# A scan kernel on one Trainium2 core: silu of two operands made 45 steps apart, projection tiles placed over the whole of a unit, D times xs made by GpSimd in place

## The chip, the core and the metric

One core of a Trainium2 chip runs the whole kernel. The metric is the device time of one execution in microseconds; the time of the kernel before is the median of three runs. The core has TensorE (PE, matmuls, with its weight loads PEld), VectorE (DVE), ScalarE (ACT), GpSimd (POOL) and SyncE (SP, which issues the DMAs); each works through its own list of instructions in program order, and they wait for one another on semaphores.

## The reference

Two batches of 1024 tokens of width 256 go through a layer with a selective scan in both directions and an MLP, and then through an attention layer with its MLP. The change touches the scan alone:

```python
xz = h @ in_w
xs, z = jnp.split(xz, 2, axis=-1)
xs = jax.nn.silu(xs)
proj = xs @ xproj_w
dt = jax.nn.softplus(proj[..., :D_INNER] + dt_bias)
Bm = proj[..., D_INNER:D_INNER + D_STATE]
Cm = proj[..., D_INNER + D_STATE:]
A = -jnp.exp(A_log)
def step(hst, ins):
    dt_t, B_t, C_t, x_t = ins
    dA = jnp.exp(dt_t[:, :, None] * A)
    hst = hst * dA + (dt_t * x_t)[:, :, None] * B_t[:, None, :]
    y_t = jnp.einsum('bds,bs->bd', hst, C_t)
    return (hst, y_t)
...
y = jnp.swapaxes(ys, 0, 1) + xs * Dskip
return y * jax.nn.silu(z) @ out_w
```

D_INNER is 512 (four groups of 128 partitions, index f), D_STATE is 64.

## The kernel before, in words

The scan is cut into 8 **units**: two directions, two batches, two halves of 512 tokens. Every second unit (1, 3, 5, 7; `hi` in the code) goes on from the state of the one before; the others start from zero. A unit has 64 **steps** `st`, one for each state; step number over all units is `w`. In each step:

- ScalarE makes four decays exp(dt x A) of 128x512 (L1091) and, between them, three copies of dtx (transposed) scaled by B for the step behind (L1073).
- TensorE turns them back into PSUM banks 4, 5 and 6 (L1652, a matmul with a diagonal that holds B, and three transposes at L1655, for each f), and adds the products of step w - 2 into banks 0 to 3 (L1661, four transposes for each f): `turn_u` and `reduce_state` in the loop at L1691.
- VectorE scans 512 tokens for each f (L1319), as soon as the decay and the PSUM bank are there. It may write step w only when TensorE has reduced step w - 3 (`RING`).
- GpSimd multiplies the scanned states by C, two f at a time (L789, 128x1024).

Beside it the **tiles** of the next unit are prepared: input path `xs` and gates `zs` (4 tiles each, 2 products each), `bc` (B and C rows, 4 products), `bT` (B turned), `dt` (4 tiles of 4 products), `dtxT` (4), and of the unit before `yT` (4) and `out` (2 tiles of 4 products). A table `TURN[u]` made by `place_turns` (L262) says at which step TensorE begins a tile; it issues one product, or one group of four transposes, in each step after f = 1 (L1700), so that a tile of four products takes four steps. All these tiles have the single PSUM bank 7 (L428), and a tile's first matmul waits until the tile before it in the bank has been copied out (`take`, `free_bank`). The copies are placed by the same table: `act_turns` (L303) puts ScalarE's copy at the end of ScalarE's step `back` = `EVICT` steps behind the start (2 for xs and zs, 3 for dt, 1 for yT, bT and dtxT), behind all decays of that step; it waits for the tile's last product. For a dt tile (L888, L889) exp follows after 4 steps (L899) and ln after 5 (L903), and GpSimd finishes dt after 6 (L766) and multiplies by xs at `DTX_STEPS` (L773). `bc` is copied by VectorE (L1200), `out` is added to x by VectorE (L1217).

In the units 1 to 6 the old table begins at step 4 with xs, yT, zs in turn (to 23), then bc 25, bT 29, dt 31, 35, 39, 43, out 47, dtxT 52, 54, 56, 58 and out 60. Once a unit, at step 24, ScalarE loads the silu table, makes silu of all xs (L919) and of all gates (L920), 128x2048 each, and loads the exp and ln table again (L1097).

D times xs comes in at a unit's first state: `first_state` (L1672) multiplies xs by a diagonal `skip_w` that holds D (L1681, fp32) for each f and c, as the first matmuls into banks 0 to 3, once VectorE has gated the unit before out of the bank (`gate_y`, L1302, in steps 1 and 2). `skip_weights` (L944) makes the eight diagonals on ScalarE at the start.

## Time and profile before

| | |
|---|---|
| median of 3 runs | 3275.02 us (3272.62 to 3275.12) |
| the profiled execution, its own time | 3272.75 us |
| its span in the profile | 3270.9 us |
| share of the span busy: PE, DVE, ACT, POOL | 98%, 88%, 86%, 71% |
| mean granted TensorE clock | 0.993 of full speed |
| first scan to last scan | 63 to 2549 us |

The profile gives for each instruction its start, its duration and the idle time of its engine before it, with the instruction that ended it in brackets. Instructions of one engine overlap a little (a scan of 1.2 us is followed by the next 1.11 us later), so what a thing costs in a full stretch is read from start to start, and short waits inside the overlap don't appear as idle time. A row of a timeline is: start (us from the span's start), us, engine, line, operation, out<-in, shapes, count, and in brackets the idle time before it and what ended it. A row of the groups by line is: line, engine, operation, names, shapes, count | busy us, mean ns of one | idle us before them, and what ended it. Matmul ends are modelled, so TensorE's busy share says little.

### The profile page before, as it was taken

What the parts mean: (1) busy time and instruction counts of PE and PEld (TensorE: products, weight loads), DVE (VectorE), ACT (ScalarE), POOL (GpSimd) and SP (SyncE); (2) the same over time, 40 slices, a digit from 0 to 9 for tenths busy, and PEclk for the clock granted to TensorE, in tenths of its full rate; (3) what the DMA queues carried; (4) which work ended last, traced back from release to release, by engine and by line L of the source; (5) the groups of instructions that cost most, each with busy time, mean ns of one, the idle gap of its engine ahead of it and who ended that gap; (6) DMA issues with size and microseconds to landing.
All of it is one profiled execution on the core that took longest, in us unless ns stands there. A gap on an engine that the chain in (4) does not pass through costs nothing.

```text
span 3270.9 us, 59384 instructions
## 1 busy us (share of the span) xinstructions
PE 3194.7 (98%) x22634; PEld 2505.6 (77%) x22634; DVE 2866.5 (88%) x2863; ACT 2815.5 (86%) x4659; POOL 2327.7 (71%) x1113
## 2 busy tenths in 40 slices
PE   8999999999999999999999999999999999999899
PEld 5888898999899998999998999999888542222244
DVE  3999999999999999999999999999999578888121
ACT  6999999999999999999999999999989436777620
POOL 1899999999999999999999999999878220000000
PEclk8999999999999999999999999999999999999999
DMA  3223222212222222222222222222212043422000
GB/s 121 69 84 81 80 72 69 72 67 72 69 73 93 70 70 75 72 69 72 73 73 74 67 72 67 74 68 71 86 57 69 29 102 59 77 34 31 15 7 20
DMA packets 199837, 218.82 MB, mean 67 GB/s; under 512 B 79969, under 2 KB 149601, under 8 KB 199297
## 3 DMA queue, kind: packets, MB, share of 16 engines
q1 hardware_dynamic: 199554, 215.02, 23.1%
q8 instruction: 180, 2.95, 0.4%
q14 instruction: 103, 0.84, 0.1%
HBM read 194.29 MB, written 18.19 MB: 65 GB/s over the span
## 4 chain that ended last, share of the span: by engine, by line
PE 76%; ACT 15%; DVE 6%; issue 3%; DMA 0%; POOL 0%; DVEq 0%; ACTq 0%; SPq 0%
PE psum L1661 21%; PE psum L1429 17%; PE psum L1655 16%; PE psum L1652 12%; ACT arena L1091 6%; ACT arena L1073 5%; PE psum L1739 4%; PE psum L1728 3%; DVE arena L1319 2%; PE psum L1712 2%; DVE row_max L1382 2%; PE psum L1681 1%; ACT arena L1116 1%; ACT arena L1076 0%; ACT arena L920 0%
## 5 line engine op out<-in xcount | busy, mean ns | idle before, releaser
L1319 DVE TENSOR_TENSOR_SCAN arena<-arena,psum 128x512 f32<-128x512 f32 x2048 | 2373.8, 1230 | 58.6 <-PE psum L1655 45.6
L789 POOL TENSOR_TENSOR arena<-arena 128x1024 f32<-128x1024 f32 x1024 | 2225.8, 2185 | 257.1 <-DVE arena L1319 233.5
L1091 ACT ACTIVATE arena<-arena,a_neg 128x512 f32<-128x512 f32 x2048 | 1442.9, 724 | 45.4 <-PE psum L1655 44.9
L1661 PE MATMUL psum<-ident,arena 128*128 128x128 f32 x8192 | 1231.9, 273 | 1.7 <-POOL arena L789 1.7
L1073 ACT ACTIVATE arena<-arena,bT 128x512 f32<-128x512 f32 x1536 | 1110.7, 723 | 0.0
L1655 PE MATMUL psum<-ident,arena 128*128 128x128 f32 x6144 | 1009.8, 273 | 0.0
L1661 PEld LDWEIGHTS psum<-ident,arena 128*128 128x128 f32 x8192 | 962.7, 141 | 2.1 <-POOL arena L789 2.1
L1652 PE MATMUL psum<-arena 128*128 128x128 f32 x4096 | 821.1, 282 | 31.8 <-ACT arena L1073 16.5
L1652 PEld LDWEIGHTS psum<-arena 128*128 128x128 f32 x4096 | 648.3, 191 | 246.6 <-issue 151.9
L1655 PEld LDWEIGHTS psum<-ident,arena 128*128 128x128 f32 x6144 | 744.2, 142 | 0.0
L1429 PE MATMUL psum<-arena 128*128 128x512 f32 (+1 forms) x1440 | 672.0, 587 | 5.2 <-DVE arena L1191 2.9
L1429 PEld LDWEIGHTS psum<-arena 128*128 128x128 f32 x1440 | 248.7, 192 | 172.4 <-issue 163.8
L1116 ACT ACTIVATE arena<-psum 128x512 f32<-128x512 f32 x512 | 267.2, 604 | 108.1 <-PE psum L1728 108.1
L1382 DVE TENSOR_REDUCE row_max<-psum 128x1 f32<-128x512 f32 x512 | 317.0, 682 | 44.8 <-PE psum L1712 44.1
L833 POOL TENSOR_TENSOR arena<-arena 128x512 f32<-128x512 f32 x8 | 10.2, 1274 | 385.5 <-DMA arena<-sums_dram 385.5
L1728 PEld LDWEIGHTS psum<-arena 100*128 100x128 bf16 x512 | 39.3, 97 | 179.1 <-ACT arena L1116 155.4
L1728 PE MATMUL psum<-arena 100*128 100x512 bf16 x512 | 160.4, 386 | 8.6 <-ACT arena L1116 6.6
L1712 PE MATMUL psum<-arena 97*128 97x512 bf16 x512 | 157.8, 386 | 6.6 <-DVE row_max L1382 6.6
L1739 PE MATMUL psum<-arena 128*32 128x512 f32 x1024 | 136.4, 604 | 4.6 <-ACT skip_w L1106 4.5
L1012 ACT ACTIVATE arena<-psum,b_up 128x512 f32<-128x512 f32 x32 | 22.0, 687 | 101.9 <-PE psum L1429 101.9
L1712 PEld LDWEIGHTS psum<-arena 97*128 97x128 bf16 x512 | 50.6, 99 | 67.9 <-DVE row_max L1382 22.3
L1233 DVE SCALAR_TENSOR_TENSOR arena<-psum,b_up,arena 128x512 f32<-128x512 f32 x32 | 24.0, 751 | 75.0 <-PE psum L1429 75.0
(118 smaller groups left out, 871.9 us busy)
## 6 DMA issues: line engine op xcount, KB each, us to landing
arena<-bc_dram SPq DMA_DIRECT2D x256, 512.0 KB, 3.7
arena<-diag_dram SPq DMA_DIRECT2D x224, 128.0 KB, 2.1
arena<-qk_dram SPq DMA_DIRECT2D x96, 128.0 KB
diag_dram<-arena SPq DMA_DIRECT2D x32, 256.0 KB, 4.4
qk_dram<-arena SPq DMA_DIRECT2D x8, 768.0 KB, 3.4
arena<-in_x SPq DMA_DIRECT2D x4, 512.0 KB, 10.5
arena<-skip_w SPq DMA_DIRECT2D x64, 32.0 KB, 2.0
arena<-sums_dram SPq DMA_DIRECT2D x64, 32.0 KB, 1.8
```

The costliest lines, as they stand in the source:

```text
L789: pool.tensor_tensor(out[:, :, way], h_now[:, :, way], c_row, ALU.mult)\
L1073: act.activation(uT[w % AHEAD][:, c - DIAGS], dtxT[:, u % 2, c], ACT.Copy, scale=bT[:, u % 2, c, st:st + 1])\
L1091: act.activation(decay[:, w % AHEAD, f], dt_[:, u % 2, f], ACT.Exp, scale=a_neg[:, d, f, st:st + 1])\
L1116: act.activation(probs[:, w % 4, jj], psum[:, n % 3, :], ACT.Exp)\
L1319: dve.tensor_tensor_scan(hs[:, w % RING, f, rows][:, way], decay[:, w % AHEAD, f, way], psum[:, 4 + n % U_BANKS, way], end_state(w - DS, f ...
L1382: dve.tensor_reduce(row_max[:, j, qt, kh:kh + 1], side_bank("scores", w), axis=AX.X, op=ALU.max)\
L1429: o = pe.matmul(dst, lhsT, rhs, start=k == 0, stop=k == len(pairs) - 1)
L1652: o = pe.matmul(dst[:, c * P:(c + 1) * P], dtxT[:, w // DS % 2, c, f * P:(f + 1) * P], diag[:, p % DIAG_PAIRS, w % 2], start=True, stop=True)
L1655: o = pe.transpose(dst[:, c * P:(c + 1) * P], uT[w % AHEAD][:, c - DIAGS, f * P:(f + 1) * P], ident[:, :])
L1661: return pe.matmul(psum[:, c, f * P:(f + 1) * P], hs[:, w % RING, f, at:at + P], ident[:, :], is_transpose=True, start=False, stop=w % DS ...
L1712: pe.matmul(take_side(pe, "scores", w), stack[u % STACKS][0:PLAIN, 0, j, qt * P:(qt + 1) * P], stack[u % STACKS][0:PLAIN, 1, j, tok(kh)], ...
L1728: pe.matmul(psum[:, n % 3, :], stack[u % STACKS][0:ROWS, 1, j, kt * P:(kt + 1) * P], stack[u % STACKS][0:ROWS, 0, j, tok(qh)], start=True, ...
```

## The change

- `place_turns`: the units 1 to 6 get another table. It begins at step 1 with zs 1, xs 3, yT 5, xs 6, yT 8, xs 9, yT 11, xs 12, yT 14, zs 15; then bc 18, dt 23, bT 27, dt 28, dt 33, zs 37, dt 39, out 44, dtxT 48, dtxT 50, zs 51, dtxT 54, dtxT 56, out 58. Units 0 and 7 keep theirs.
- silu: in units 1 to 6 ScalarE makes silu of xs at step 15 and silu of the gates at step 60, each between its own pair of table loads. In units 0 and 7 it stays at steps 24 and 18.
- D times xs: `scale_skip` on GpSimd multiplies xs by D in place, four times a unit (steps 48, 50, 60, 62 of the unit before, and before the first product for unit 0), after dtx has been made from it. TensorE adds xs by four transposes for each f (`turn_skip`): f = 0 at the first state, 1 to 3 at the states 1 to 3. `skip_w`, `skip_weights` and the fp32 matmuls are gone.
- GpSimd's `DTX_STEPS` become 40, 44, 49, 52 (unit 0 keeps 40, 44, 53, 55).

```diff
-SILU_STEP, LAST_SILU_STEP = 24, 18
+FIRST_SILU_STEP, XS_SILU_STEP, GATE_SILU_STEP, LAST_SILU_STEP = 24, 15, 60, 18
-DTX_STEPS = (40, 44, 53, 55)
+FIRST_DTX_STEPS, DTX_STEPS = (40, 44, 53, 55), (40, 44, 49, 52)
+SKIP_STEPS = (48, 50, 60, 62)
...
-            else:
-                place([step for k in range(NI) for step in (xs_[k], yT_[k], zs_[k])], 4)
-            at[BC_TURN] = ("bc", u + 1)
-            at[BT_TURN] = ("bT", u + 1)
...
+            place([zs_[0], xs_[0], yT_[0], xs_[1], yT_[1], xs_[2], yT_[2], xs_[3], yT_[3], zs_[1]], 1)
+            place([("bc", u + 1)], 18)
+            place([("dt", u + 1, 0), ("bT", u + 1), ("dt", u + 1, 1)], 23)
+            place([("dt", u + 1, 2), zs_[2], ("dt", u + 1, 3)], 33)
+            place([("out", u - 1, 0), ("dtxT", u + 1, 0)], 44)
+            place([("dtxT", u + 1, 1), zs_[3]], 50)
+            place([("dtxT", u + 1, 2)], 54)
+            place([("dtxT", u + 1, 3)], 56)
+            place([("out", u - 1, 1)], 58)
...
-            if st == (LAST_SILU_STEP if u == UNITS - 1 else SILU_STEP):
-                todo.append(("silu", u + 1))
+            if u in (0, UNITS - 1):
+                if st == (LAST_SILU_STEP if u else FIRST_SILU_STEP):
+                    todo.append(("silu", u + 1, u == 0, True))
+            elif st == XS_SILU_STEP:
+                todo.append(("silu", u + 1, True, False))
+            elif st == GATE_SILU_STEP:
+                todo.append(("silu", u + 1, False, True))
...
+            def scale_skip(u, f):
+
+
+                pool.tensor_scalar(xs[:, f], xs[:, f], d_skip[:, unit(u)[0], f:f + 1], 0.0, ALU.mult, ALU.add).then_inc(s["skip_ready"], 1)
...
+                    if st in SKIP_STEPS and u < UNITS - 1:
+                        f = SKIP_STEPS.index(st)
+                        pool.wait_ge(s["dtx_ready"], NI * (u + 1) + f + 1)
+                        pool.wait_ge(s["tile_full"], first["dt", u + 1, NI - 1] + 1)
+                        scale_skip(u + 1, f)
...
-            def silu(u):
-
-                act.wait_ge(s["tile_free_act"], eaten(first["zs", u - 1, TB - 1], "a"))
-                if u < UNITS:
+            def silu(u, paths, gates_too):
+
+                if paths:
+                    act.wait_ge(s["tile_free_act"], eaten(first["xs", u, NI - 1], "a"))
                     act.activation(xs, xs, ACT.Silu).then_inc(s["silu_ready"], 1)
...
+            def turn_skip(u, f, c):
+
+                if c == 0:
+                    pe.wait_ge(s["skip_ready"], NI * u + f + 1)
+                pe.matmul(psum[:, c, f * P:(f + 1) * P], xs[:, f, c * P:(c + 1) * P], ident[:, :],
+                          is_transpose=True, start=False, stop=False)
+
             def reduce_state(w, f):
 
+
+                st = w % DS
+                if f == 0 and st < NI:
+                    for c in range(TB):
+                        turn_skip(w // DS, st, c)
...
                 for f in range(NI):
-                    pe.matmul(psum[:, c, f * P:(f + 1) * P], xs[:, f, c * P:(c + 1) * P],
-                              skip_w[:, unit(u)[0], f], start=f == 0, stop=False)
-                for f in range(NI):
                     o = turn_h(w, f, c)
+                turn_skip(u, 0, c)
```

Three places show how instructions moved. Lines are those of each file: L1450, L1523, L1673, L1676, L1682 of the changed kernel are L1429, L1502, L1652, L1655, L1661 of the one before, and on ScalarE L915, L916, L926, L930, L963, L1094, L1112 are L888, L889, L899, L903, L934, L1073, L1091.

TensorE, unit 1, from the bT tile (transposes of `bc_rows`) to the first product of the next dt tile (`arena<-...128x512`). Before:

```order
L1502 MATMUL psum<-ident,bc_rows 128x128 [waits bc_rows_ready]
L1502 MATMUL psum<-ident,bc_rows 128x128 x3
L1652 MATMUL psum<-arena 128x128 [waits scan_done]
...
L1652 MATMUL psum<-arena 128x128 [waits scan_done,diag_in_1,uT_ready]
...
L1652 MATMUL psum<-arena 128x128 [waits scan_done,uT_ready]
...
L1429 MATMUL psum<-arena 128x512 [waits tile_free_act,silu_ready]
```

and now:

```order
L1523 MATMUL psum<-ident,bc_rows 128x128 [waits tile_free_act,bc_rows_ready]
L1523 MATMUL psum<-ident,bc_rows 128x128 x3
L1673 MATMUL psum<-arena 128x128 [waits scan_done]
...
L1673 MATMUL psum<-arena 128x128 [waits scan_done,diag_in_0,uT_ready]
...
L1450 MATMUL psum<-arena 128x512 [waits tile_free_act,silu_ready]
```

`uT_ready` is waited for once a step, at f = 0: two steps began between bT and the dt product before, one now.

ScalarE at the same place in the changed kernel: the two copies of the first dt tile, the exp, the copy of bT and the ln, with the seven decays and scaled copies of a step between them:

```order
L915 ACTIVATE arena<-psum,dt_bias 128x512 [waits tile_full]
L916 ACTIVATE arena<-psum,dt_bias 128x512
L1112 ACTIVATE arena<-arena,a_neg 128x512 [waits scan_done]
...
L926 ACTIVATE arena<-arena 128x512 [waits tile_free_act]
...
L963 ACTIVATE bT<-psum 128x256 [waits tile_full]
L930 ACTIVATE arena<-arena 128x512 [waits exp_step]
```

The bT copy used to stand one step and more ahead of the first dt tile's copies; now it stands two steps behind them.

GpSimd, steps 48 to 52 of unit 1 in the changed kernel: L811 are the products by C (two a step), L790 is D times xs, L782 makes dtx.

```order
L790 TENSOR_SCALAR arena<-arena,d_skip 128x512 [waits tile_full,dtx_ready]
L811 TENSOR_TENSOR arena<-arena 128x2x512 [waits scan_done] x2
L782 TENSOR_TENSOR arena<-arena 128x512 [waits tile_full,dt_ready]
L811 TENSOR_TENSOR arena<-arena 128x2x512 [waits scan_done,c_in_1]
L811 TENSOR_TENSOR arena<-arena 128x2x512 [waits scan_done]
L790 TENSOR_SCALAR arena<-arena,d_skip 128x512 [waits tile_full,dtx_ready]
L811 TENSOR_TENSOR arena<-arena 128x2x512 [waits scan_done] x2
L811 TENSOR_TENSOR arena<-arena 128x2x512 [waits scan_done,c_in_0]
L811 TENSOR_TENSOR arena<-arena 128x2x512 [waits scan_done]
L782 TENSOR_TENSOR arena<-arena 128x512 [waits tile_full,dt_ready]
```

The L790 rows have no counterpart in the kernel before; its dtx products stand at steps 53 and 55, with no extra at 48 to 52 but one L766 at 49.

## Rows read from the trace of the kernel before

**Rows 1.** The page: busy us (share of the span) xinstructions

```profile
PE 3194.7 (98%) x22634; PEld 2505.6 (77%) x22634; DVE 2866.5 (88%) x2863; ACT 2815.5 (86%) x4659; POOL 2327.7 (71%) x1113
```

**Rows 2.** Timeline of VectorE: the first gate of units 2 to 4

```profile
702.90 0.69 DVE L1302 TENSOR_TENSOR arena<-psum,arena 128x512 f32<-128x512 f32 x1 [0.23 <-PE psum L1661]
...
1006.84 0.69 DVE L1302 TENSOR_TENSOR arena<-psum,arena 128x512 f32<-128x512 f32 x1 [0.17 <-PE psum L1661]
...
1314.08 0.69 DVE L1302 TENSOR_TENSOR arena<-psum,arena 128x512 f32<-128x512 f32 x1 [0.23 <-PE psum L1661]
```

**Rows 3.** Timeline of VectorE, scans in units 2 and 3

```profile
949.29 11.20 DVE L1319 TENSOR_TENSOR_SCAN arena<-arena,psum 128x512 f32<-128x512 f32 x10
...
1019.80 10.63 DVE L1319 TENSOR_TENSOR_SCAN arena<-arena,psum 128x512 f32<-128x512 f32 x9
```

**Rows 4.** Timeline of TensorE, unit 2, first dt tile

```profile
858.85 1.02 PE L1429 MATMUL psum<-arena 128*128 128x512 f32 x2
859.71 0.38 PE L1652 MATMUL psum<-arena 128*128 128x128 f32 x2
...
863.66 0.59 PE L1429 MATMUL psum<-arena 128*128 128x512 f32 x1
```

**Rows 5.** Timeline of TensorE, the bT tile and the first state of unit 2

```profile
835.68 0.60 PE L1502 MATMUL psum<-ident,bc_rows 128*128 128x128 f32 x4
...
705.63 1.06 PE L1681 MATMUL psum<-skip_w,arena 128*128 128x128 f32 x8
```

**Rows 6.** Timeline of ScalarE behind the first dt tile, unit 2

```profile
859.91 0.69 ACT L888 ACTIVATE arena<-psum,dt_bias 128x512 f32<-128x512 f32 x1 [1.87 <-PE psum L1429]
...
865.36 0.62 ACT L899 ACTIVATE arena<-arena 128x512 f32<-128x512 f32 x1
865.88 1.33 ACT L1091 ACTIVATE arena<-arena,a_neg 128x512 f32<-128x512 f32 x2
...
870.18 0.62 ACT L903 ACTIVATE arena<-arena 128x512 f32<-128x512 f32 x1
```

**Rows 7.** Timeline of ScalarE, the silu block of unit 1

```profile
501.66 1.28 ACT L919 ACT_TABLE_LOAD   x1
502.96 1.92 ACT L919 ACTIVATE arena<-arena 128x2048 f32<-128x2048 f32 x1
...
507.99 1.33 ACT L1091 ACTIVATE arena<-arena,a_neg 128x512 f32<-128x512 f32 x2
```

**Rows 8.** Timeline of VectorE, unit 2, at silu and dt

```profile
815.53 6.93 DVE L1319 TENSOR_TENSOR_SCAN arena<-arena,psum 128x512 f32<-128x512 f32 x6 [0.73 <-ACT arena L1091]
...
839.87 15.64 DVE L1319 TENSOR_TENSOR_SCAN arena<-arena,psum 128x512 f32<-128x512 f32 x14
```

**Rows 9.** Timeline of ScalarE at the start of the kernel

```profile
31.05 2.43 ACT L948 ACTIVATE skip_w<-ident,d_skip 128x128 f32<-128x128 f32 x8
```

**Rows 10.** Groups by line, whole span

```profile
L1661 PE MATMUL psum<-ident,arena 128*128 128x128 f32 x8192 | 1231.9, 273 | 1.7 <-POOL arena L789 1.7
...
L1429 PE MATMUL psum<-arena 128*128 128x512 f32 (+1 forms) x1440 | 672.0, 587 | 5.2 <-DVE arena L1191 2.9 <-ACT skip_w L1106 0.7 <-ACT arena L876 0.7
...
L773 POOL TENSOR_TENSOR arena<-arena 128x512 f32<-128x512 f32 x28 | 36.0, 1286 | 0.0
...
L941 ACT ACTIVATE arena<-psum 128x512 f32<-128x512 f32 x32 | 18.3, 584 | 0.0
...
L934 ACT ACTIVATE bT<-psum 128x256 f32<-128x256 f32 x8 | 2.9, 364 | 0.0
```

**Rows 11.** GpSimd, unit 4 by line; its timeline

```profile
L789 POOL TENSOR_TENSOR arena<-arena 128x1024 f32<-128x1024 f32 x129 | 278.4, 2172 | 18.0 <-DVE arena L1319 14.2
...
967.10 19.32 POOL L789 TENSOR_TENSOR arena<-arena 128x1024 f32<-128x1024 f32 x9
```

**Rows 12.** SyncE's timeline at 1295 and the DMA view (KB each, us to landing)

```profile
1295.55 0.47 SPq L546 DMA_DIRECT2D arena<-in_bwd_in_w  x1
...
arena<-in_bwd_in_w SPq DMA_DIRECT2D x2, 512.0 KB, 4.1
```

42 lines of the change are left out of this document (21 added, 21 removed).

## Prediction, made before the changed kernel ran

> **What bounds the kernel now.** Read the page first. TensorE, VectorE and ScalarE are each busy 86 to 98% of the span [rows 1], which only says that no single one can be blamed, so the next view is the stretch that repeats: units 1 to 6 of the scan, 64 steps each, where all edits but one lie. The first output gate of a unit, in its step 1, marks it [rows 2]: from mark to mark it is 307.24 us where the unit carries a state on (units 1, 3, 5: "carrying") and 303.94 where it starts from zero (2, 4, 6: "fresh"). Six of them are 1834 us of the span.
>
> What one step costs each engine comes from start-to-start times. VectorE: ten scans of a fresh unit start within 11.20 us less the last one's 1.20, 1.11 each, 4.45 a step; nine of a carrying unit within 10.63 less 1.26, 1.17 each, 4.69 a step [rows 3]. TensorE: from one piece of a projection to the same point a step later is 858.85 to 863.66, 4.81 us; the piece itself is 0.86 of it (858.85 to 859.71; its row says 1.02, so a group's last 0.16 overlaps the next), and a bare step is 3.95. A transposed tile of four is 0.60 less that overlap, 0.44: 4.39 with its step [rows 4, 5]. ScalarE: four decays and three scaled copies take 4.30 (865.88 to 870.18) [rows 6].
>
> A fresh unit asks of TensorE 64 x 3.95 = 252.8, 44 pieces x 0.86 = 37.8, 9 transposed tiles x 0.44 = 4.0, and at its first state four times 1.06 less 0.16 for D times xs [rows 5] = 3.6: 298.2 of 303.9. TensorE is the bound there, and loses 5.7. A carrying unit asks of VectorE 64 x 4.69 = 300.2, plus four gates, a copy and two output additions at about 0.6 each, 4.2: 304.4 of 307.2. VectorE bounds it, and loses 2.8. ScalarE's demand is 64 x 4.30 = 275.2, 33 evictions and softplus steps of about 0.5 each, 16.3, and the silu block of 6.33 (501.66 to 507.99) [rows 7]: 297.8. So three engines stand within 2% of each other, and what decides is who waits for whom inside a step. TensorE can run ahead by three PSUM banks: three steps ahead of the piece at 858.85, at 844.4, the first dt piece begins, and VectorE scans without a pause to 855.5 [rows 8], past the second and third. Two pieces x (4.81 - 4.45): I estimate the lead at 0.7 to 0.8 us.
>
> **What the change removes.** D times xs goes from 16 fp32 matmuls of two passes to 16 single-pass transposes: 3.6 becomes 16 x 0.11 = 1.8 a unit, 1.8 of TensorE's demand, worth up to 1.8 in a fresh unit and nothing in a carrying one. The 8 scaled copies of the identity leave ScalarE at the start, 2.43 us [rows 9], which bounds the gain; TensorE's first dt tile, four pieces of 0.86, runs through it, so I take 0. The silu block of 6.33 no longer falls on one step: now VectorE idles 0.73 for a decay behind it [rows 8]; with what TensorE loses beside, I estimate 0.9 a unit comes back.
>
> **What it adds on ScalarE.** One more pair of table loads a unit, 2 x 1.30 = 2.6 (501.66 to 502.96) [rows 7]: 297.8 becomes 300.4, still under both unit lengths. The xs silu at step 15 is a block of 1.30 + 1.92 + 1.30 = 4.5, smaller than the 6.3 that costs 0.9 today, and meets the same lead: nothing. The gates' silu at step 60 is 4.5 too, but ScalarE reaches it just after the late evictions; it is followed by two to three gates (about 2 us of VectorE time that needs no decay), so I put it at 0 to 2.5 and take 0. The Trainium skill, ScalarE: Activation LUTs, sections What ACT_TABLE_LOAD costs and Table sets: the hidden batching unit, speaks against the split: batch by set, and budget about 2.66 us for each switch with its drain. The rows show 1.30 from the load's start to the next instruction, so this trace does not agree with the page on the drain; by the page the pair would be 5.3 and ScalarE's demand 303.1, 2.7 more than I use.
>
> **What it adds on GpSimd.** Four in-place multiplications of 128x512 a unit. Nothing like them is in the trace: a 128x512 product of two tensors is 1.29 [rows 10], a 128x1024 one 2.17 [rows 11]. I take 1.29, the same size, and keep 0 (all of it hidden) to 2.2 each. GpSimd idles 18 in a fresh unit before its products [rows 11], so 5.2 fit. Locally steps 48, 49, 50 and 52 now carry one extra each: 4 x 1.24 less what a step leaves over two products (4.81 - 4.28 beside a piece, 4.45 - 4.28 bare; nine products start within 19.32 less 2.17, 2.14 each [rows 11]) is a lag of about 3 to 3.5. Today TensorE waits for products only 1.7 us in the whole run [rows 10]. A product has a step (4.45) less itself (2.17), and TensorE's own distance, before it is missed: about 2.3 to 4. Taken: 0; at 2.2 us each, 1 to 2 us a unit.
>
> **What moving the tiles does.** This is the term that decides. All projection tiles of a unit use one PSUM bank, so a tile's first matmul waits until its predecessor has been copied out. ScalarE copies in its own program order, after the decays of a fixed step, and for dt only after the tile's last piece is done. Before, a bare step stood between bT (29) and the first dt tile (31), and the four dt tiles followed each other. Now bT sits between two dt tiles without a gap, a gate tile between two others, and a gate tile right behind a dtxT tile. Three chains follow, counted from the start of a dt tile's last piece:
>
> - *Step 28.* ScalarE copies at +1.06, ends its next step at +6.51 (865.36), does exp, and ends the one after at +11.33 (870.18) [rows 6]; only then comes the bT copy, 0.36 [rows 10]: +11.7. TensorE wants the bank after one step with a piece and one with bT, 4.81 + 4.39 = +9.2. It waits **2.5**. A ScalarE lead cannot help: it is itself tied to the dt piece, where it already waits 1.87 today [rows 6].
> - *Step 39.* The gate tile of steps 37 and 38 is copied after +11.33, ln 0.52 and one more step 4.30, plus 0.58 for the copy [rows 10]: +16.7. TensorE is there at 3 x 4.81 = +14.4. It waits 2.3, or up to 2.8 if ScalarE is late at step 36 (five steps with exp and ln, 24.7, against 24.3): **2.5**.
> - *Step 51.* After the last dt piece (42): +11.85 at step 44, seven steps of 4.30, two dtxT copies of 0.5: +43.0. TensorE needs 9 x 3.95 + 5 x 0.86 + 2 x 0.44 = 40.7, and VectorE holds it to some 41.1 in a fresh unit, 42.0 in a carrying one. It waits **1.9** or **1.0**.
>
> **The sum.** Fresh: 298.2 - 1.8 + 6.9 of these waits, and of today's 5.7 lost all but 0.9 (silu) and 0.5 (bare steps are spread): 4.3. That is 307.6 against 303.9, +3.7. Carrying: VectorE feels each wait less the lead, 1.7 + 2.4 + 0.2 = 4.3; back come 0.9 (silu) and about 0.7 since the 20 pieces in a row are broken up: 309.9 against 307.2, +2.7. Three of each: +19.2. Units 0 and 7 keep their tables; there, at the start and behind the scan I count 0. The gate tiles of unit 4 now want the other direction's weights at step 1 instead of 7; SyncE issues them at 1295.55, they land in 4.1 and the unit's step 1 is at 1314 [rows 2, 12]: 0, with 14 us to spare. The profiled execution took 3272.75 us (span 3270.9), 2.3 below the median of the runs, 3275.02; the sum gives 3292 from the one and 3294 from the other. I say **3293**, with 3284 to 3304 as this case's own range (ordinary losses 2 us a unit less, GpSimd's or the late silu's price more).
>
> **Rivals.** A measurement here can tell about 0.2%, 6.5 us, from no change.
> 1. *The spread pays* (faster). If ScalarE got its copies out in time, the three waits were near zero, TensorE would need 296.4 + 4.3 in a fresh unit, -3.2, and carrying units would lose 1.2 instead of 2.8, -1.6: 3 x 4.8 = 14 less, **3261**. It decides where the waits are under 2 us a unit together. For it: between xs, yT and gate tiles a copy and the next tile share a step today and TensorE's waits before products, 5.2 us in all [rows 10], name none of these copies. Against it: there ScalarE is not tied to a just finished dt piece, and at 28 and 39 it is. Chance 0.11.
> 2. *GpSimd late on top* (slower still): 1.5 us x 6 more, **3302**. For it the four extras in five steps; against it 18 us of idle. Chance 0.08.
> 3. *ScalarE binds* and the waits mostly vanish in its own lateness, while the gates' silu costs 2.5 in fresh units: 300.4 + 2.5 there, -1.0, carrying -0.5: **3270**, no change. By the Trainium skill's figure above it would be 303.1 + 2.5 there, +1.7 instead of -1.0. Chance 0.09.
> 4. That the edit doesn't do what it says: a transpose of xs could still take two passes, 1.8 a unit; inside the range.
>
> **How the numbers follow.** Forecast 0.72, rivals 0.11, 0.08, 0.09. Slower by over 0.2% (above 3281.5) takes forecast and rival 2: 0.80; rival 3 is 0.09; faster 0.11. The range 3274 to 3304 leaves out rival 1 and part of 3.
>
> **What would show it.** Units of about 310 and 307.5 between gate marks. TensorE waiting 2 to 2.7 us for the bT copy once in each of six units, as much for a gate tile's copy at 39, less at 51; VectorE idle 4 to 5 in carrying and about 14 in fresh units, put down to TensorE. ScalarE waiting for the dt pieces of steps 26, 31 and 42 in each unit. The D matmul line gone, 128 transposes of 0.11 instead. I am wrong if TensorE shows no wait for those copies, or if the first waits end on a product of GpSimd or on the silu at step 60.

## The result, and the profile after

The changed kernel takes 3314.28 us, the median of 4 runs (3310.20 to 3315.04), against 3273.82 for the kernel before (4 runs, 3272.40 to 3275.12): a ratio of 1.0119, interval 1.0106 to 1.0132. It is slower, as forecast, but by 40 us instead of 19, and outside both ranges of the prediction (3284 to 3304, and 3274 to 3304). The profiled execution took 3314.05 us (span 3312.3, before 3270.9).

The page, busy us (share of the span) xinstructions, against [rows 1]:

```profile
PE 3191.7 (96%) x22506; PEld 2497.4 (75%) x22506; DVE 2863.7 (86%) x2863; ACT 2827.7 (85%) x4663; POOL 2348.1 (71%) x1145
```

No engine has much more to do: TensorE 3 us less, ScalarE 12 more, GpSimd 20 more. The 41 us are idle time. VectorE's first gates of units 2, 3 and 4, the **marks** of [rows 2]; lengths of units below run from mark to mark. (The texts stated before each run also have lengths from a unit's first scan to the next unit's, which differ by 0.1 to 0.7 us.)

```profile
714.01 0.69 DVE L1323 TENSOR_TENSOR arena<-psum,arena 128x512 f32<-128x512 f32 x1 [0.84 <-PE psum L1682]
...
1023.59 0.69 DVE L1323 TENSOR_TENSOR arena<-psum,arena 128x512 f32<-128x512 f32 x1 [0.67 <-PE psum L1682]
...
1336.02 0.69 DVE L1323 TENSOR_TENSOR arena<-psum,arena 128x512 f32<-128x512 f32 x1 [0.84 <-PE psum L1682]
```

The fresh unit is 309.58 us long (303.94 before), the carrying one 312.43 (307.24): +5.64 and +5.19, where +3.7 and +2.7 had been forecast. The gate itself now waits 0.84 us for TensorE's last reduce instead of 0.23.

Groups by line over the whole span, against [rows 10]:

```profile
L1340 DVE TENSOR_TENSOR_SCAN arena<-arena,psum 128x512 f32<-128x512 f32 x2048 | 2370.5, 1228 | 92.5 <-PE psum L1676 79.3 <-ACT arena L1112 10.7 <-PE psum L1682 0.4
...
L1450 PE MATMUL psum<-arena 128*128 128x512 f32 (+1 forms) x1440 | 673.5, 589 | 44.8 <-ACT arena L940 17.8 <-ACT bT L963 14.9 <-ACT arena L957 7.2
...
L915 ACT ACTIVATE arena<-psum,dt_bias 128x512 f32<-128x512 f32 x28 | 19.3, 690 | 51.3 <-PE psum L1450 51.3
L790 POOL TENSOR_SCALAR arena<-arena,d_skip 128x512 f32<-128x512 f32 x32 | 23.9, 749 | 57.0 <-DVE arena L1229 57.0
L1689 PE MATMUL psum<-ident,arena 128*128 128x128 f32 x128 | 23.1, 273 | 0.0
```

TensorE's products waited 5.2 us in the whole run before and 44.8 now, for three copies of ScalarE: the gate tile's (L940), bT's (L963) and dtxT's (L957). bT's is 2.48 us in each of six units. TensorE's timeline shows the waits of steps 28, 39 and 51 in unit 4:

```profile
1465.86 1.10 PE L1450 MATMUL psum<-arena 128*128 128x512 f32 x2 [2.48 <-ACT bT L963]
...
1520.89 1.10 PE L1450 MATMUL psum<-arena 128*128 128x512 f32 x2 [2.75 <-ACT arena L940]
...
1578.51 1.10 PE L1450 MATMUL psum<-arena 128*128 128x512 f32 x2 [1.71 <-ACT arena L957]
```

And ScalarE's chain to the first of them, as [rows 6] gave it: the copy of the dt tile waits for its last product, exp follows one step later, bT's copy after one more:

```profile
1455.08 0.69 ACT L915 ACTIVATE arena<-psum,dt_bias 128x512 f32<-128x512 f32 x1 [2.54 <-PE psum L1450]
...
1460.53 0.62 ACT L926 ACTIVATE arena<-arena 128x512 f32<-128x512 f32 x1
...
1465.34 0.37 ACT L963 ACTIVATE bT<-psum 128x256 f32<-128x256 f32 x1
```

So the chains of the forecast stand, near their length. What was wrong had to be sought in what VectorE makes of them and in what lies beside them. VectorE around step 28, first in the carrying unit 3, then in the fresh unit 4:

```profile
1138.83 15.32 DVE L1340 TENSOR_TENSOR_SCAN arena<-arena,psum 128x512 f32<-128x512 f32 x13
1156.38 9.60 DVE L1340 TENSOR_TENSOR_SCAN arena<-arena,psum 128x512 f32<-128x512 f32 x8 [2.24 <-PE psum L1676]
...
1450.92 4.55 DVE L1340 TENSOR_TENSOR_SCAN arena<-arena,psum 128x512 f32<-128x512 f32 x4 [0.25 <-PE psum L1676]
1455.72 9.00 DVE L1340 TENSOR_TENSOR_SCAN arena<-arena,psum 128x512 f32<-128x512 f32 x8 [0.26 <-PE psum L1676]
1467.64 4.55 DVE L1340 TENSOR_TENSOR_SCAN arena<-arena,psum 128x512 f32<-128x512 f32 x4 [2.91 <-PE psum L1676]
```

In the carrying unit VectorE stands 2.24 us, and the 0.1 us of overlap between two scans is gone as well, for a wait of 2.48: 0.1 of it is absorbed, where the forecast had 0.7 to 0.8. In the fresh unit VectorE already waits 0.25 us in each step with a piece before it comes.

### The profile page after: what moved, and what is told of

Same layout as the page of the kernel before. It is cut to its first block, busy times and chain, and to the rows that moved or that the text cites. A ratio compares the mean times of both kernels' runs of the same rounds, so it can differ in the third digit from the quotient of the medians.

```text
span 3312.3 us, 59192 instructions
## 1 busy us (share of the span) xinstructions
PE 3191.7 (96%) x22506; PEld 2497.4 (75%) x22506; DVE 2863.7 (86%) x2863; ACT 2827.7 (85%) x4663; POOL 2348.1 (71%) x1145
## 4 chain that ended last, share of the span: by engine, by line
PE 61%; ACT 26%; DVE 7%; issue 5%; DMA 0%; POOL 0%; DVEq 0%; ACTq 0%; SPq 0%
PE psum L1450 16%; PE psum L1682 15%; ACT arena L1112 12%; PE psum L1676 12%; ACT arena L1094 9%; PE psum L1673 9%; DVE arena L1340 4%; PE psum L1769 4%; PE psum L1758 3%; PE psum L1742 2%; DVE row_max L1403 2%; ACT arena L1137 1%; DVE arena L1323 0%; ACT arena L1097 0%; ACT arena L916 0%
## 5 line engine op out<-in xcount | busy, mean ns | idle before, releaser
L811 POOL TENSOR_TENSOR arena<-arena 128x1024 f32<-128x1024 f32 x1024 | 2225.0, 2190 | 218.3 <-DVE arena L1340 198.9
L1112 ACT ACTIVATE arena<-arena,a_neg 128x512 f32<-128x512 f32 x2048 | 1432.3, 719 | 27.5 <-PE psum L1676 27.0
L1682 PE MATMUL psum<-ident,arena 128*128 128x128 f32 x8192 | 1234.3, 274 | 3.0 <-POOL arena L811 1.6
L1094 ACT ACTIVATE arena<-arena,bT 128x512 f32<-128x512 f32 x1536 | 1104.7, 719 | 0.0
L1676 PE MATMUL psum<-ident,arena 128*128 128x128 f32 x6144 | 1010.9, 274 | 0.0
L1682 PEld LDWEIGHTS psum<-ident,arena 128*128 128x128 f32 x8192 | 963.5, 142 | 5.2 <-DVE arena L1323 3.0
L1673 PE MATMUL psum<-arena 128*128 128x128 f32 x4096 | 818.7, 282 | 35.0 <-DVE arena L1340 21.5
L1673 PEld LDWEIGHTS psum<-arena 128*128 128x128 f32 x4096 | 649.3, 191 | 247.4 <-issue 155.0
L1676 PEld LDWEIGHTS psum<-ident,arena 128*128 128x128 f32 x6144 | 745.1, 142 | 0.0
L1450 PE MATMUL psum<-arena 128*128 128x512 f32 (+1 forms) x1440 | 673.5, 589 | 44.8 <-ACT arena L940 17.8
L1450 PEld LDWEIGHTS psum<-arena 128*128 128x128 f32 x1440 | 248.7, 192 | 215.8 <-issue 207.2
```

The lines of the kernel that those rows point to most:

```text
L811: pool.tensor_tensor(out[:, :, way], h_now[:, :, way], c_row, ALU.mult)\
L1094: act.activation(uT[w % AHEAD][:, c - DIAGS], dtxT[:, u % 2, c], ACT.Copy, scale=bT[:, u % 2, c, st:st + 1])\
L1112: act.activation(decay[:, w % AHEAD, f], dt_[:, u % 2, f], ACT.Exp, scale=a_neg[:, d, f, st:st + 1])\
L1450: o = pe.matmul(dst, lhsT, rhs, start=k == 0, stop=k == len(pairs) - 1)
L1673: o = pe.matmul(dst[:, c * P:(c + 1) * P], dtxT[:, w // DS % 2, c, f * P:(f + 1) * P], diag[:, p % DIAG_PAIRS, w % 2], start=True, stop=True)
L1676: o = pe.transpose(dst[:, c * P:(c + 1) * P], uT[w % AHEAD][:, c - DIAGS, f * P:(f + 1) * P], ident[:, :])
```

## Experiments

The first four were stated together, after this reading; e5, e6, e7 and c1 after their results; e8, e9, e10 and c2 after those. In the texts, "the change" is the changed kernel, and tables are those of the units 1 to 6. A **step** of VectorE is counted from its first scan to the first scan of the next step. A **fall of the clock** is a stretch in which TensorE's granted clock is at half its full level; the last section is about it, and it lengthens a unit by some 1.6 us.

**e1_bt_early**: bT in front of the dt tiles, so that the wait of step 28 has no cause.

```diff
-            place([("dt", u + 1, 0), ("bT", u + 1), ("dt", u + 1, 1)], 23)
+            place([("bT", u + 1)], 22)
+            place([("dt", u + 1, 0), ("dt", u + 1, 1)], 24)
```

> The changed kernel with bT moved from between the first two dt tiles (27) to the step behind bc (22), dt at 24 and 28; all else as changed. Theory A, the copies of a tile that come too late for the next tile in the one bank (TensorE delayed by 2.6 us at step 28 in each unit): that delay goes, VectorE gets back 2.4 in units 1, 3, 5 and 2.7 in units 2, 4, 6, 15 us in all: 3299. Rival B, ScalarE's demand (300.4 us a unit with its extra table loads) is the bound and the wait only shows it: under 3 us come back, 3311 or more. Rival C, the extra GpSimd work delays the products: nothing changes, 3314.

Measured: 3302.54 us (3300.46 to 3305.27), ratio 1.0089, interval 1.0074 to 1.0104: 11.7 less than the change. The wait for bT is gone from TensorE's row and those for the gate tile's and dtxT's copies remain. Theory A, short of its 15 us: the clock falls in five units here, and in two of the changed kernel. Like against like, unit 5 (no fall in either) is 309.91 against 312.20, and unit 6 (a fall in both) 308.22 against 310.76: 2.3 and 2.5 less for a wait of 2.48.

**e2_gates_last**: the gate tile behind the dt tiles, so that step 39 has no wait.

```diff
-            place([("dt", u + 1, 2), zs_[2], ("dt", u + 1, 3)], 33)
+            place([("dt", u + 1, 2), ("dt", u + 1, 3), zs_[2]], 33)
```

> The changed kernel with the gate tile of step 37 moved behind the last dt tile (dt 33 and 37, gates 41); the tile order is otherwise the changed one. Theory A: the delay at step 39 (2.9 us of TensorE) goes, 3.1 and 3.0 us a unit, 18 us in all: 3296; the waits at 28 and 51 stay as they are. Rival B: under 3 us. Rival C: nothing, or slower, as the last dt is done two steps earlier for GpSimd.

Measured: 3294.60 us (3291.99 to 3297.23), ratio 1.0064, interval 1.0049 to 1.0079. Theory A; 19.7 less than the change for one place, since the wait behind step 50 shrinks with it (TensorE's row: 14.9 us for bT and 4.6 for dtxT, of 7.2).

**e3_no_copy_waits**: both, and a bare step between dtxT and the last gate tile.

```diff
-            place([("dtxT", u + 1, 1), zs_[3]], 50)
-            place([("dtxT", u + 1, 2)], 54)
-            place([("dtxT", u + 1, 3)], 56)
-            place([("out", u - 1, 1)], 58)
+            place([("dtxT", u + 1, 1)], 50)
+            place([zs_[3]], 52)
+            place([("dtxT", u + 1, 2)], 55)
+            place([("dtxT", u + 1, 3)], 57)
+            place([("out", u - 1, 1)], 59)
```

> The changed kernel with all three neighbours parted: bT at 22, dt 24, 28, 33, 37, gates 41, and behind dtxT 50 one free step before the last gate tile (52), dtxT 55 and 57, out 59. Silu at 15 and 60 and D times xs on GpSimd as changed. Theory A: 15 + 18 + 5 us come back, 3276, units of about 307 and 303; no wait of TensorE for a copy over 0.5 us is left behind step 16. Rival B: ScalarE's 300.4 a unit plus its waits for dt pieces holds the units over 308 and 305, 3290 or more. Rival C: TensorE waits for products of GpSimd about steps 50 to 55 in place of the copies.

Measured: 3279.08 us (3276.22 to 3282.65), ratio 1.0015, interval 1.0005 to 1.0024: 35.2 of the 40 us go with the copy waits. Marks of units 2, 3 and 4:

```profile
705.16 0.69 DVE L1325 TENSOR_TENSOR arena<-psum,arena 128x512 f32<-128x512 f32 x1 [0.85 <-PE psum L1684]
...
1010.07 0.69 DVE L1325 TENSOR_TENSOR arena<-psum,arena 128x512 f32<-128x512 f32 x1 [0.67 <-PE psum L1684]
...
1317.11 0.69 DVE L1325 TENSOR_TENSOR arena<-psum,arena 128x512 f32<-128x512 f32 x1 [0.84 <-PE psum L1684]
```

TensorE's products, group by line over the whole span:

```profile
L1452 PE MATMUL psum<-arena 128*128 128x512 f32 (+1 forms) x1440 | 671.6, 587 | 7.5 <-DVE arena L1214 2.9 <-ACT arena L942 2.5 <-ACT attn_sb L1129 0.7
```

304.91 and 307.04: 4.67 and 5.39 less than in the change. The carrying unit is now at its old length, the fresh one still 1.0 over, and the gates still wait 0.85 and 0.67.

**e4_d_alone**: the tables and the silu block of before, with D times xs as in the change (GpSimd in place, transposes at the states 0 to 3).

```diff
-            place([zs_[0], xs_[0], yT_[0], xs_[1], yT_[1], xs_[2], yT_[2], xs_[3], yT_[3], zs_[1]], 1)
...
+            place([step for k in range(NI) for step in (xs_[k], yT_[k], zs_[k])], 4)
```

> The kernel before with one part of the change alone: D times xs by GpSimd in place and turned by TensorE, no diagonals; tile table, silu block and dtx steps as before. Prediction's term: 1.8 us of TensorE in each of the units 2, 4, 6, nothing in 1, 3, 5: 5.4 us less, 3268. If GpSimd's four extras are felt (rival C), 1 to 2 us a unit more instead, 3275 to 3285, with TensorE waiting for products. If the transposes of xs are felt where they stand now (steps 3 to 5, beside tiles of this table only at 4 and 5), half the gain goes, 3271.

Measured: 3281.30 us (3278.44 to 3282.15), ratio 1.0019, interval 1.0009 to 1.0028. A miss for the theory of a gain: the step that was to save TensorE 1.8 us a unit costs 0.88 in a fresh and 0.69 in a carrying one (marks 707.10, 1011.92, 1319.85). VectorE just behind the gates, units 3 and 4:

```profile
1017.84 15.33 DVE L1332 TENSOR_TENSOR_SCAN arena<-arena,psum 128x512 f32<-128x512 f32 x13
1033.38 7.19 DVE L1332 TENSOR_TENSOR_SCAN arena<-arena,psum 128x512 f32<-128x512 f32 x6 [0.21 <-PE psum L1668]
...
1325.58 14.62 DVE L1332 TENSOR_TENSOR_SCAN arena<-arena,psum 128x512 f32<-128x512 f32 x13
1340.82 9.00 DVE L1332 TENSOR_TENSOR_SCAN arena<-arena,psum 128x512 f32<-128x512 f32 x8 [0.62 <-PE psum L1668]
```

Where the transposes of xs (0.44) stand beside a piece (0.86), TensorE's step is 3.95 + 0.86 + 0.44 = 5.25 by the prediction's prices, and VectorE's step 5 in unit 4 takes 5.25 (5.01 in unit 3).

**e5_split_alone**: e4 with the silu block cut in two, at steps 24 and 60.

```diff
-                if st == (LAST_SILU_STEP if u == UNITS - 1 else FIRST_SILU_STEP):
-                    todo.append(("silu", u + 1, u < UNITS - 1, True))
...
+            elif st == FIRST_SILU_STEP:
+                todo.append(("silu", u + 1, True, False))
+            elif st == GATE_SILU_STEP:
+                todo.append(("silu", u + 1, False, True))
```

> The tiles keep their steps of before, D times xs is the change's own (as in e4_d_alone, 3281 us, units 308.3 and 304.4), and the silu block of step 24 is cut in two: silu of xs at step 24, silu of the gates at step 60, each between its own table loads. Theory A (each block of 4.5 us costs only what is over ScalarE's lead): the block at step 24 shrinks from 6.3 to 4.5 us and gives back up to 0.9 us a unit at steps 24 to 26; the one at step 60 costs a fresh unit 1.6 (0.9 and 0.7 over 4.45 at two steps in the changed kernel's unit 4) and a carrying one 0.6. Sum per pair of units about +0.5: 3281 to 3285 us. Theory B (the second pair of table loads costs its 2.6 us in each unit, as ScalarE has no lead left): units 310.9 and 307.0, 3296 us. Theory C (the split pays because the big block is broken up): 3276 us.

Measured: 3285.25 us (3281.68 to 3286.74), ratio 1.0033, interval 1.0020 to 1.0046. By total theory A, by its parts not: carrying units are unchanged (unit 3 307.89, e4 307.92), and fresh ones are 1.8 to 1.9 longer (306.58). In unit 4, steps 24 to 26 give back 1.4 us, and steps 60 to 62 take 3.3 more. In the carrying unit 5, steps 24 to 28 give back 1.1 and steps 60 to 63 take 0.9 more. VectorE in unit 2, behind the block at step 60:

```profile
979.30 6.75 DVE L1337 TENSOR_TENSOR_SCAN arena<-arena,psum 128x512 f32<-128x512 f32 x6
988.83 6.92 DVE L1337 TENSOR_TENSOR_SCAN arena<-arena,psum 128x512 f32<-128x512 f32 x6 [2.79 <-ACT arena L1109]
```

**e6_d_first_state**: e4 with all sixteen transposes of xs in the first state.

```diff
-                if f == 0 and st < NI:
-                    for c in range(TB):
-                        turn_skip(w // DS, st, c)
...
-                turn_skip(u, 0, c)
+                for f in range(NI):
+                    turn_skip(u, f, c)
```

> Tiles and silu as before; D times xs by GpSimd, and all sixteen transposes of xs in the first state, where VectorE gates and TensorE has time, instead of four there and four at each of the states 1 to 3. Theory A (e4_d_alone's 0.7 to 0.9 us a unit come only from transposes beside a piece at steps 4 and 5): units back at 307.5 and 303.7, 3274 us, or 3277 if the scan again starts some 3 us later for TensorE's clock. Theory B (VectorE's gates bound there and TensorE's time counts behind them): the 1.8 us less of TensorE in a fresh unit show, 306.9 and 302.5, 3268 us. Theory C (the loss is GpSimd's products, late behind the four multiplications, not the transposes): units stay at 308.3 and 304.4, 3281 us, and TensorE waits for products.

Measured: 3274.56 us (3271.51 to 3275.80), ratio 1.0002, interval 0.9992 to 1.0011. Theory A: units of 303.99 and 307.24 between marks, as before. In unit 3 VectorE goes through 22 scans where e4's stops after 13:

```profile
1014.80 25.86 DVE L1332 TENSOR_TENSOR_SCAN arena<-arena,psum 128x512 f32<-128x512 f32 x22
```

Two things follow. GpSimd's four products a unit are wholly hidden, and their cost is 0: TensorE waits for products of GpSimd 2.7 us in the whole run (before: 1.7), so no price of theirs stands against a gain. And the 1.8 us less on TensorE is worth nothing; the fp32 matmuls stood between VectorE's gates, which take the same time without them (steps 1 and 2 of unit 4 are 6.57 and 5.06 long, before 6.58 and 5.06).

**e7_spread_from_2**: e3 with e6's first state, and its table up to the second dt tile one step later, so that no piece stands before the last reduce of the unit before (the silu of xs goes along, from step 15 to 16).

```diff
-            place([zs_[0], xs_[0], yT_[0], xs_[1], yT_[1], xs_[2], yT_[2], xs_[3], yT_[3], zs_[1]], 1)
-            place([("bc", u + 1)], 18)
+            place([zs_[0], xs_[0], yT_[0], xs_[1], yT_[1], xs_[2], yT_[2], xs_[3], yT_[3], zs_[1]], 2)
+            place([("bc", u + 1)], 19)
```

> e3_no_copy_waits (3279 us; no tile of it wants the bank before its copy is out) with two more repairs: all transposes of xs in the first state, and the table begins at step 2 instead of 1, so that no piece stands before the last reduce of the unit before. Theory A (the first gate late by 0.5 us at step 1 and 0.9 to 1.1 us at steps 4 to 6 are what is left beside the silu of the gates): units of about 306 and 303.2, 3270 us (3267 to 3273). Theory B (the losses come from the load of ScalarE or GpSimd, not from the two places): as e3_no_copy_waits, 3276 to 3280 us. Theory C (a block at step 60 in fresh units, 1.6 us, and dips of TensorE's clock eat it up): 3275 us with steps 60 to 62 above 5 us in units 2, 4 and 6.

Measured: 3271.90 us (3268.19 to 3277.00), ratio 0.9996, interval 0.9987 to 1.0006. Units of 303.62 and 305.88: 1.29 and 1.16 less than e3's, as theory A had it for the two places. The fresh units also show what theory C named: steps 60 to 62 of unit 4 are 6.75, 4.95 and 5.37 us long, 3.7 over three of 4.44. Of this, 1.4 is not the block's: the out tile and VectorE's addition stand there, and e9 below, with no block at step 60, has 4.44, 4.88 and 5.37. ScalarE's timeline near the end of unit 2:

```profile
979.47 1.28 ACT L951 ACT_TABLE_LOAD   x1
980.76 1.92 ACT L951 ACTIVATE arena<-arena 128x2048 f32<-128x2048 f32 x1
982.69 1.28 ACT L1120 ACT_TABLE_LOAD   x1
```

VectorE's, there:

```profile
974.73 7.91 DVE L1342 TENSOR_TENSOR_SCAN arena<-arena,psum 128x512 f32<-128x512 f32 x7
984.80 6.93 DVE L1342 TENSOR_TENSOR_SCAN arena<-arena,psum 128x512 f32<-128x512 f32 x6 [2.16 <-ACT arena L1114]
992.23 2.33 DVE L1342 TENSOR_TENSOR_SCAN arena<-arena,psum 128x512 f32<-128x512 f32 x2 [0.50 <-PE psum L1678]
```

VectorE runs out of decays at 982.64, 3.2 us after the block of 4.5 began. ScalarE's lead there, taken as this time, is shorter than the block.

**c1_before_again**: the kernel before, unchanged.

> The kernel before once more, unchanged, for its start. In the profiles so far the first scan starts at 63.4 us (before), 67.7 (changed), 64.7, 64.6, 65.5 and 67.3 (experiments whose instructions up to there are all the same as in the changed kernel). Theory A (TensorE's clock comes up at a moment that differs from execution to execution): this profile may start its scan anywhere from 63 to 68 us, at the same granted clock rows that go with it. Theory B (the missing diagonals or another part of the changed start make it late): 63.4 again, with full clock at 10 us.

Measured: 3274.22 us in one run; the first scan starts at 64.97 us, not 63.43. Theory A, so far as one profile can show it.

**e8_gates_at_47**: e7 with the last gate tile at 44 and the silu of the gates at 47.

```diff
-FIRST_SILU_STEP, XS_SILU_STEP, GATE_SILU_STEP, LAST_SILU_STEP = 24, 16, 60, 18
+FIRST_SILU_STEP, XS_SILU_STEP, GATE_SILU_STEP, LAST_SILU_STEP = 24, 16, 47, 18
-FIRST_DTX_STEPS, DTX_STEPS = (40, 44, 53, 55), (40, 44, 49, 52)
+FIRST_DTX_STEPS, DTX_STEPS = (40, 44, 53, 55), (40, 44, 52, 54)
...
-            place([("out", u - 1, 0), ("dtxT", u + 1, 0)], 44)
-            place([("dtxT", u + 1, 1)], 50)
-            place([zs_[3]], 52)
+            place([zs_[3], ("out", u - 1, 0)], 44)
+            place([("dtxT", u + 1, 0)], 51)
+            place([("dtxT", u + 1, 1)], 53)
```

> e7_spread_from_2 (3272 us, units 306.2 and 303.3) with the last gate tile moved from step 52 to 44 and the silu of the gates from step 60 to 47, into the stretch where each step holds a piece (4.81 us) and ScalarE's 4.30 leaves it half a microsecond a step; out moves to 46, the first two dtxT to 51 and 53. In e7 the block at step 60 makes steps 60 to 62 of unit 4 6.75, 4.95 and 5.37 us long over 4.44, 3.7 us. Theory A (the block costs there because ScalarE has no lead left behind the late copies, and is hidden where a piece makes steps longer): fresh units 299.6 to 300.5, carrying 305.6, 3261 to 3264 us. Theory B (a block of 4.5 us costs wherever it stands, about 1.6 fresh and 0.6 carrying): 3267 to 3269 us. Theory C (the late dtxT tiles make GpSimd or TensorE wait): 3272 us or more.

Measured: 3284.16 us (3280.03 to 3286.26), ratio 1.0026, interval 1.0015 to 1.0036. Slower, as theory C had it, but in the main for none of the reasons given: the fault of the change was built in again. The out tile at step 46 stands right behind the gate tile of 44 and 45, whose copy ScalarE makes behind its step 46:

```profile
920.21 1.10 PE L1452 MATMUL psum<-arena 128*128 128x512 f32 x2 [2.08 <-ACT arena L942]
```

Between xs, yT and gate tiles at the start of a unit the same neighbours cost nothing. Here ScalarE had been tied to the dt tiles' last products until step 40, which may be why; no run parts it. The wait is not the whole loss: steps 44 to 50 of unit 5 take 36.9 us against 33.6 in e7, 3.3 more for a wait of 2.08, and those of unit 4 3.8 more. So about 1.2 to 1.7 us are lost beside the wait, and the block begins at step 47; what part of it is the block's this run doesn't tell.

**e9_gates_at_0**: e7 with the silu of the gates at the end of ScalarE's step 0 of the next unit.

```diff
-            elif st == GATE_SILU_STEP:
-                todo.append(("silu", u + 1, False, True))
+            if u >= 2 and st == 0:
+                todo.append(("silu", u, False, True))
```

> e7_spread_from_2 with the silu of the gates moved from step 60 to the end of ScalarE's step 0 of the next unit, just ahead of VectorE's four gates in steps 1 and 2. Theory A (the gates, some 2 us in which VectorE needs no decay, cover the block, as the prediction had it for step 60): fresh units 300 us, 3262 us. Theory B (the decays of step 1 are late before the gates begin, so the gates cover only what follows): the 2.3 us of the first step stay, the 1.4 behind it go, fresh 301.9, carrying unchanged, 3267 us. Theory C (the first gate waits for the silu too and TensorE's first state behind it): step 1 above 9 us, 3272 us or more.

Measured: 3262.34 us (3261.34 to 3263.80), ratio 0.9962, interval 0.9946 to 0.9977, 13 us faster than the kernel before (3275.33 by the 11 executions beside it). Theory A by its number, with units of 301.50 and 306.18. Its reason was another. ScalarE's timeline at the end of unit 2:

```profile
997.80 1.28 ACT L951 ACT_TABLE_LOAD   x1
999.10 1.92 ACT L951 ACTIVATE arena<-arena 128x2048 f32<-128x2048 f32 x1
1001.03 1.28 ACT L1120 ACT_TABLE_LOAD   x1
```

VectorE's, there:

```profile
994.00 11.70 DVE L1342 TENSOR_TENSOR_SCAN arena<-arena,psum 128x512 f32<-128x512 f32 x10
1005.87 0.69 DVE L1325 TENSOR_TENSOR arena<-psum,arena 128x512 f32<-128x512 f32 x1 [0.17 <-PE psum L1684]
```

VectorE scans without a stop through the block and comes to its first gate 3.6 us after it is over. It is not the gates that cover the block: four steps after step 60 ScalarE has lead enough for 4.5 us again. Carrying units pay 0.3 for the block at this place.

**e10_bt_between_alone**: the kernel before with bT between two dt tiles, and nothing else.

```diff
+            if u:
+                at[BT_TURN] = ("dt", u + 1, 0)
+                place([("bT", u + 1), ("dt", u + 1, 1), ("dt", u + 1, 2), ("dt", u + 1, 3)], BT_TURN + 4)
             for f in range(NI):
-                at[DT_TURN + 4 * f] = ("dt", u + 1, f)
+                if not u:
+                    at[DT_TURN + 4 * f] = ("dt", 1, f)
```

> The kernel before with one chain of the change alone: the first dt tile at step 29, bT right behind it at 33, and the other dt tiles at 34, 38 and 42, so that bT stands between two dt tiles without a gap; silu, D times xs and all else as before (units 307.5 and 303.7). TensorE should wait 2.5 us for bT's copy at step 34. Theory A (VectorE feels the wait in full, since TensorE comes to it without a lead behind four pieces): step 34 or the one behind it 2.3 to 3 us longer than its neighbours, units up by 2.3 (carrying) and up to 3 (fresh), 3286 to 3290 us. Theory B (the prediction's: TensorE's lead of 0.7 to 0.8 us takes part of it): carrying +1.7, fresh +2.5 at most, 3284 to 3287 us with carrying units at 309.2. Theory C (ScalarE's copy is early enough without the other tiles' copies): 3275 us. In carrying units the three differ by 0.6 and 1.7 us, and the profile tells that.

Measured: 3297.85 us (3297.36 to 3298.46), ratio 1.0071, interval 1.0057 to 1.0084, more than each theory gave. TensorE's wait in unit 3:

```profile
1177.47 1.10 PE L1433 MATMUL psum<-arena 128*128 128x512 f32 x2 [2.48 <-ACT bT L938]
```

VectorE's timeline beside it, and the marks that close unit 2 and unit 3:

```profile
1150.90 25.91 DVE L1323 TENSOR_TENSOR_SCAN arena<-arena,psum 128x512 f32<-128x512 f32 x22
1179.25 10.90 DVE L1323 TENSOR_TENSOR_SCAN arena<-arena,psum 128x512 f32<-128x512 f32 x9 [2.44 <-PE psum L1659]
...
1017.76 0.69 DVE L1306 TENSOR_TENSOR arena<-psum,arena 128x512 f32<-128x512 f32 x1 [0.17 <-PE psum L1665]
...
1327.19 0.69 DVE L1306 TENSOR_TENSOR arena<-psum,arena 128x512 f32<-128x512 f32 x1 [0.23 <-PE psum L1665]
```

Here VectorE had scanned 22 times without a stop, so TensorE was not behind, and still the wait arrives whole: step 34 of unit 3 takes 7.40 us between steps of 4.69, and the unit is 309.43, 2.19 over 307.24 where theory B allowed 1.7. Theory A. The fresh unit 2 is 4.25 longer (308.19), more than the wait; the clock fell in it, as in units 1, 4 and 6, which is why the total is over every theory.

**c2_changed_again**: the changed kernel, unchanged.

> The changed kernel once more, unchanged, for the places where TensorE's granted clock falls to 0.5 for 3.4 us. In its first profile that was at 587 and 2144 us, in units 1 and 6, which are 1.7 to 2 us longer than their fellows. Theory A (a wait of 2.5 us and more lets the clock fall when it meets a certain moment, which differs from execution to execution): other units, or none, are hit here, and the units not hit are 312.4 and 309.4 us again; the start of the scan anywhere from 63 to 68 us. Theory B (it belongs to those places of the program): units 1 and 6 again.

Measured: 3309.43 us in one run. The granted clock falls at 895.6, 1151.6 and 1209.6 us, in units 2 and 3, not 1 and 6. Its units 4, 5 and 6, without a fall, are 309.55, 312.19 and 309.10 long; in the first profile 4 and 5, without one, were 309.60 and 312.20. Theory A. The scan starts at 64.61 us, not 67.66.

## Why the prediction was wrong in size

All times here are between marks, of units 2 and 3, in which none of these profiles shows a fall of the clock. The chain of kernels divides the difference:

| from | to | fresh | carrying | what lies between |
|---|---|---|---|---|
| before | e9 | -2.44 | -1.06 | tiles spread without a copy wait, silu block divided, D by GpSimd in the first state |
| e9 | e7 | +2.12 | -0.30 | silu of the gates at step 60 |
| e7 | e3 | +1.29 | +1.16 | a piece at step 1, xs transposes beside pieces |
| e3 | changed | +4.67 | +5.39 | the three copy waits |
| before | changed | +5.64 | +5.19 | |

Three of each are 32.5 us, against 19.2 in the forecast. Put beside the forecast's terms:

| term | forecast, fresh and carrying | measured, fresh and carrying |
|---|---|---|
| D times xs, and the table's first step (e7 to e3) | -1.8, 0 | +1.29, +1.16 |
| copy waits and the silu at step 60 (e9 to e7, e3 to changed) | +6.9, +4.3 | +6.79, +5.09 |
| what comes back (before to e9) | -1.4, -1.6 | -2.44, -1.06 |

Of the 13.3 us between 19.2 and 32.5 the first row makes 12.8, the second 2.0, and the third takes 1.5 back. Step by step:

- *D times xs: the step that failed.* The forecast took 1.8 us off a fresh unit and 0 off a carrying one. **The sign was wrong**: nothing comes back (e6), and the transposes at the states 1 to 3 cost 0.88 and 0.69 (e4). I had counted demand over the unit, where the place decides: sixteen fp32 matmuls in the shadow of four gates are free, four transposes beside a piece are not. That zs begins at step 1, before the last reduce of the unit before, I had not priced at all; it makes the first gate 0.5 to 0.6 us late.
- *The copy waits.* Right in place and length: 2.5, 2.5 and 1.9 us were forecast for a fresh unit, and unit 4 has 2.48, 2.75 and 1.71. The last was to be 1.0 in a carrying one; the view of waits has 2.4 for units 3 and 4 together, so 0.7. **Mis-sized was what a carrying unit feels of them**, "each wait less the lead", 1.7 + 2.4 + 0.2 = 4.3 (only 0.1 was taken off at step 39); it is 5.39. In unit 3 step 28 takes 7.04 against 4.69 in e3, step 39 7.75 against 4.81, and steps 51 and 52 together 0.5 more: 2.35, 2.94 and 0.5. A lead of 0.7 to 0.8 us was worked out from a stretch in which VectorE ran on over two pieces. By e10 nothing of it is there against such a wait. Why is not shown. One reading is that pieces stand right before and behind the wait, each with a step of 4.81 of TensorE against 4.69 of VectorE, and that a lead which is used up there does not help at the wait; no run tested it.
- *GpSimd.* Taken at 1.29 us a product and 0 for the time. The product is 0.75 us, and the time 0 (e6). The Trainium skill, GPSIMD Engine Reference, section 3.1, has 768 ns for 512 elements of a tight loop at its best, and names the second input as what makes `tensor_tensor` slower. The trace agrees, with 0.75 us for one input and 1.29 for two: my 1.29 was a row with two inputs. The rival of a late GpSimd was wrong: TensorE waits for its products 1.6 us in the whole changed run.
- *The gates' silu.* Put at 0 to 2.5, taken as 0, since gates follow it. In the changed kernel 0 is about right: steps 60 to 63 of unit 4 take 19.38 us together, against 19.14 in the kernel before and 19.15 in e9, neither of which has a block there; those of unit 3 19.39 against 19.40 before. But the reason given was wrong, and it was luck. In e3 and e7, without the copy waits, the block costs a fresh unit 2.1. What goes with the cost is ScalarE's lead. In e7 it is 3.2 us from the block's start to VectorE's stop, behind four late copies. In the changed kernel it is 4.85, about the block's 4.5; ScalarE's and VectorE's rows in unit 4:

```profile
1618.49 1.28 ACT L949 ACT_TABLE_LOAD   x1
```

```profile
1621.01 2.33 DVE L1340 TENSOR_TENSOR_SCAN arena<-arena,psum 128x512 f32<-128x512 f32 x2 [0.25 <-PE psum L1676]
1623.82 4.55 DVE L1340 TENSOR_TENSOR_SCAN arena<-arena,psum 128x512 f32<-128x512 f32 x4 [0.48 <-ACT arena L1112]
```

  That TensorE's waits gave ScalarE this lead back, or that its last copy stands one step further ahead of the block than in e3, are both possible; no run parts them. So the 2.12 of the chain's second row is not paid in the changed kernel, its three waits (6.94 us) cost a fresh unit about 6.8 and not 4.67, and "6.9" was right for fresh units. The table loads are as the rows had them: from the load's start to the silu's 1.29 us, and the second load 1.28. The Trainium skill, ScalarE: Activation LUTs, section What ACT_TABLE_LOAD costs, would have about 2.66 for each switch with its drain; this trace still does not agree with it on the drain.
- *What comes back.* 0.9 and 0.5 or 0.7 were forecast, and -2.44 and -1.06 is what the spread and the divided block bring once nothing waits (e9): a fresh unit gets more back than forecast, a carrying one less, and the sum hides it. The rival "The spread pays" had -3.2 and -1.6, 3261 us, and e9 takes 3262. That is luck in part: its -3.2 holds the 1.8 for D times xs that is worth nothing, and e9 has the gates' silu at another place.
- *Start, unit 0, unit 7, behind the scan*: 0 forecast. In the profiled execution the scan starts 4.2 us later, units 1 to 6 together are 34.9 longer, 2.4 more than the table's 32.5, with two falls of the clock in them, units 0 and 7 are 0.4 shorter, and what lies behind unit 7 is 2.7 longer. The sum is 41.4, as between the two spans. By c1 (64.97 us) and c2 (64.61) the start need not be the change's, and behind unit 7 c2 has 1.0 and not 2.7.

So the direction came from three chains that were read right. The missing half came from a credit for TensorE where it was not the bound, with the transposes and the first gate tile that it was traded for, then from what carrying units feel of the waits, the falls of the clock, and a start that came late in that profile.

## What to carry to other kernels

A tile's place in such a table has a price that depends on its neighbours in the same bank: put behind a tile whose copy is tied to its own last product, it waits by the length of the copying engine's program, and nearly the whole wait arrives at the bounding engine (2.2 to 2.9 us here for waits of 2.5 to 2.75). Give such tiles a bare step or another kind of tile between; e8 shows how easily one is missed. Demand saved on an engine counts only at the steps where that engine sets the pace. And a block on an engine that runs ahead is free only where its lead is longer than the block: read it as the time from the block's start to the stop of the one who waits, place by place, as at 979.47 and 982.64 in e7 (2.1 us lost) and at 1618.49 and 1623.34 in the changed kernel (0.2).
